# Mixing the blocks of one weight's Hadamard transform on GpSimd instead of TensorE, in a transformer layer's kernel

## The reference

```python
x = x + _layernorm(attn(_layernorm(x)))       # 16 heads of 32, rotary on all of q and k
x = x + _layernorm(ffn(_layernorm(x)))
# ffn, with n = 512, INTER = 2048:
x = fwht(x * SU_ug) / SCALE
x_up = x @ W_up.T * (Wscale_ug[:INTER] * SCALE)
x_gate = x @ W_gate.T * (Wscale_ug[INTER:] * SCALE)
x = jax.nn.silu(x_gate) * x_up
x = fwht(x * SU_dp) / SCALE
x = x @ W_down.T * (Wscale_dp * SCALE)
```

## Time and profile before

| what | us |
|---|---|
| median of 3 runs (1948.71 to 1949.36) | 1949.24 |
| time of the profiled execution | 1946.86 |
| its span | 1944.8 |
| PE busy | 1845.8 |
| DVE busy | 1263.3 |
| ACT busy | 1159.8 |
| POOL busy | 940.5 |

### The profile page before, as it was taken

One profiled execution on the slowest core, in us unless ns is written; L12 is line 12 of the kernel. 1 busy time (PEld: TensorE's weight loads), 2 busy tenths in 40 slices (PEclk: granted clock), 3 DMA queues, 4 the chain that ended last, 5 costly groups with the idle time before them and its releaser, 6 DMA issues.

```text
span 1944.8 us, 45513 instructions
## 1 busy us (share of the span) xinstructions
PE 1845.8 (95%) x18248; PEld 1282.4 (66%) x18248; DVE 1263.3 (65%) x2477; ACT 1159.8 (60%) x2003; POOL 940.5 (48%) x990
## 2 busy tenths in 40 slices
...
GB/s 245 248 99 132 157 55 61 99 142 93 72 88 145 91 98 126 98 126 99 89 114 142 87 73 93 135 100 99 118 106 126 99 88 107 112 76 77 119 84 71
DMA packets 353009, 213.23 MB, mean 110 GB/s; under 512 B 285216, under 2 KB 286496, under 8 KB 351776
## 3 DMA queue, kind: packets, MB, share of 16 engines
...
## 4 chain that ended last, share of the span: by engine, by line
PE 73%; DVE 8%; ACT 6%; POOL 4%; issue 4%; DMA 3%; SPq 1%; POOLq 0%; ACTq 0%; DVEq 0%
PE ps L900 29%; PE ps L925 15%; PE ps L846 5%; PE ps L836 5%; PE ps L857 5%; PE ps L873 4%; PE ps L892 2%; PE ps L747 2%; PE ps L878 2%; DVE mx L1385 2%; PE ps L805 2%; ACT pr L1076 1%; POOL rs L1470 1%; DMA qT<-tok 1%; POOL pr L1496 1%
## 5 line engine op out<-in xcount | busy, mean ns | idle before, releaser
L1076 ACT ACTIVATE pr<-ps,exp_scale 128x512 f16<-128x512 f32 x512 | 352.0, 688 | 262.1 <-PE ps L857 252.9
L1496 POOL TENSOR_TENSOR pr<-p,pr 128x512 f16<-128x512 f32 x256 | 296.4, 1158 | 326.5 <-ACT p L1082 326.4
L1385 DVE TENSOR_REDUCE mx<-ps 128x1 f32<-128x512 f32 x512 | 333.2, 683 | 97.7 <-PE ps L846 95.6
L900 PE MATMUL ps<-x2T,gate_w 128*128 128x256 f16 x3072 | 377.5, 273 | 0.0
L900 PE MATMUL ps<-x2T,up_w 128*128 128x256 f16 x3072 | 377.2, 273 | 0.0
L925 PE MATMUL ps<-room 128*128 128x512 f16 x1536 | 363.4, 379 | 0.2
L1399 DVE TENSOR_TENSOR pr<-ps,pr 128x512 f16<-128x512 f32 x256 | 176.1, 688 | 257.8 <-ACT ps L1087 257.5
L900 PEld LDWEIGHTS ps<-x2T,gate_w 128*128 128x128 f16 x3072 | 298.1, 98 | 56.7 <-issue 4.4
L900 PEld LDWEIGHTS ps<-x2T,up_w 128*128 128x128 f16 x3072 | 300.2, 98 | 43.2
L1524 POOL TENSOR_TENSOR room<-room 128x256 f16<-128x256 f32 x256 | 170.9, 676 | 273.2 <-ACT room L1112 272.9
L925 PEld LDWEIGHTS ps<-room 128*128 128x128 f16 x1536 | 148.4, 98 | 158.3 <-POOL room L1524 6.2
...
## 6 DMA issues: line engine op xcount, KB each, us to landing
room<-down_mid SPq DMA_DIRECT2D x256, 256.0 KB, 3.0
...
x2T<-in_W_gate SPq DMA_DIRECT2D x5, 1024.0 KB, 5.8
gate_w<-in_W_down SPq DMA_DIRECT2D x4, 1024.0 KB, 7.5
```

Source lines behind the costliest of these rows:

```text
L900: mm = nc.tensor.matmul(ffn_ps[i % 2][:, half * HALF:(half + 1) * HALF], weights[:, chunks[j // 4], kt, pw, j % 4 * P:(j % 4 + 1) * P], x2 ...
L1076: nc.scalar.activation(pr[:, p_buf(b, U), 0, 2 * j:2 * j + 2, :].rearrange("p h q -> p (h q)"), work[k], ACT.Exp, scale=exp_scale[:, 0:1]) ...
L1385: nc.vector.tensor_reduce(mx[:, t, h:h + 1], work[k], AX.X, ALU.max).then_inc(sm_freed.sem, 1)
L1496: nc.gpsimd.tensor_tensor(lo, p32[:], hi, ALU.subtract).then_inc(p_low.sem, 1)
```

## The change

After it, chunks 0 to 3 of W_down are loaded once, to the four parts of up_w. mx reads them there. A new POOL step bf does H(4) over m1 in fp32: for the widths 512 and 1024 it adds and subtracts halves, from `raw[k]` to `mid` and back, each time 1024 columns wide. cut then works on mixed numbers. dz has two matmuls. The halves from dyh and dyl go to a buffer of their own, `d_turned`, with two places. ldx.0 to 3 are gone; raw.0 to 3 wait for nothing. Chunks 4 and on use other buffers and waits, and all tables of order and of PSUM banks are new.

```diff
+MIX = (4 * P, 8 * P)
...
-        RAW_AT = [gate_part(2), gate_part(0), gate_part(1), gate_part(2), gate_part(0), gate_part(2), gate_part(0), gate_part(2),
-                  x2_16, gate_part(0), x2_16, x2_16]
-        CUT_AT = [up_part(c) for c in range(4)] + [gate_part(1), up_part(3), gate_part(1), up_part(3)] + [
+        RAW_AT = [up_part(c) for c in range(4)] + [gate_part(0), x2_16, gate_part(0), x2_16, gate_part(0), x2_16, x2_16, x2_16]
+        CUT_AT = [gate_part(2), up_part(0), up_part(1), up_part(2)] + [gate_part(1), up_part(3), gate_part(1), up_part(3)] + [
...
+        mid = gate_part(3).bitcast(F32)
...
+        d_turned = room[:, 3072:4096].bitcast(F16).rearrange("p (k i n) -> p k i n", k=2, i=2)
...
             def ldx(b, k):
-                if k >= 2:
+                if k >= 6:
                     sp.wait_ge(m_seen, k - 1)
...
             def raw_(b, k):
-                if k < 3:
-                    sp.wait_ge(a_lo, 4 * k + 4)
...
+                if k < 4:
+                    sp.dma_start(raw[k], chunk(k)).then_inc(d_in[k], 16)
...
             def dz(b, n):
-                pe.wait_ge(t_done, 4 * (n // 4) + 4)
-                mixed(n, n % 4)
+                pe.wait_ge(t_done, n + 1)
+                if n == 0:
+                    pe.wait_ge(bo_sum, 2)
+                if n >= 2:
+                    pe.wait_ge(q_done, n - 1)
+                for i in range(2):
+                    mm = nc.tensor.matmul(ps[:, 6 + n % 2, :], had[0], d_turned[:, n % 2, i, :], start=i == 0, stop=i == 1)
+                mm.then_inc(q_filled, 1)
...
             def cut_(b, k):
-                sc.wait_ge(r_loaded[k % 3], 16 * (k // 3 + 1))
-                sc.wait_ge(d_scaled if k < 4 else f_scaled, 1)
+                if k < 4:
+                    sc.wait_ge(d_mixed, k + 1)
+                    sc.wait_ge(d_scaled, 1)
+                    if k == 0:
+                        sc.wait_ge(a_lo, 4)
+                    if k:
+                        sc.wait_ge(d_lo, k)
...
             def mx_(b, k):
+                if k < 4:
+                    dve.wait_ge(d_in[k], 16)
...
+            def bf(b, k):
+
+                pool.wait_ge(d_in[k], 16)
+                for n, width in enumerate(MIX):
+                    src, dst = ((raw[k], mid), (mid, raw[k]))[n % 2]
+                    left, right = (src.rearrange("p (m i n) -> p m i n", i=2, n=width)[:, :, i, :] for i in range(2))
+                    both = dst.rearrange("p (m i n) -> p m i n", i=2, n=width)
+                    if n == 0 and k:
+                        pool.wait_ge(d_mixed, k)
+                    if n:
+                        pool.wait_ge(d_turn, (len(MIX) - 1) * k + n)
+                    if n == 1:
+                        pool.wait_ge(m_seen, k + 1)
+                    nc.gpsimd.tensor_tensor(both[:, :, 0, :], left, right, ALU.add)
+                    nc.gpsimd.tensor_tensor(both[:, :, 1, :], left, right, ALU.subtract).then_inc(
+                        d_mixed if n == len(MIX) - 1 else d_turn, 1)
```

The beginnings of the new FRONT of POOL, SP, ACT and PE (those of before in the first lines of each pair):

```diff
-        xs.0 xs.1 xs.2 xs.3 xn.0 xn.1 xn.2 xn.3 asl.0 asl.1 asl.2 asl.3 asl.4 xs.0@1 asl.5 asl.6 asl.7 asl.8
-        asl.9 asl.10 proj.0.0 ...
+        xs.0 xs.1 xs.2 xs.3 xn.0 xn.1 bf.0 xn.2 asl.0 asl.1 asl.2 asl.3 asl.4 asl.5 asl.6 xn.3 bf.1 asl.7 asl.8
+        asl.9 asl.10 asl.11 bf.2 proj.0.0 cut.0 tok.0.0 proj.0.1 cut.1 tok.0.1 bf.3 proj.1.0 cut.2 xs.0@1
+        tok.1.0 cut.3 proj.1.1 ...
...
-        xl.0 xl.1 lda.4 lda.2 ldv.2 xl.2 xl.3 lda.3 lda.1 lda.5 ldx.0 ldv.0 lda.0 ldx.1 ln1.0 xl.0@1 ln1.1 ldx.2
-        ln1.2 ln1.3 ldv.3 ldx.3 ...
+        lda.4 lda.2 xl.0 xl.1 xl.2 ldv.2 lda.3 lda.1 lda.5 xl.3 ldv.0 raw.0 lda.0 raw.1 ln1.0 raw.2 raw.3 ldv.3
+        ldv.4 ldx.4 xl.0@1 ln1.1 ln1.2 ldv.1 ldx.5 ln1.3 wput.0 ldx.6 xl.1@1 wget.0 ldx.7 ...
...
+        xn.0 xn.1 xn.2 ash.0 ash.1 ash.2 ash.3 ash.4 ash.5 ash.6 xn.3 arh ash.7 ash.8 ash.9 ash.10 brh ash.11
+        c.1 cut.0 tk.0.0 c.0 cut.1 tk.0.1 cut.2 v.0 v.1 tk.1.0 cut.3 ...
...
-        ... smax.0.15 warm.7 v.2 v.3 dy.0 warm.3 dy.1 st.0 st.1 dy.2 st.2 ...
+        ... smax.0.15 warm.4 proj.1.1 warm.10 v.2 v.3 st.0 st.1 dy.0 dy.1 dz.0 st.2 ...
```

More of the change, by code:

```diff
@@ L61 @@
     PE="""
[L62 to L85, removed]
+        smax.3.4 c.1@1 smax.3.5 av.18 av.19 smax.3.6 smax.3.7 c.0@1 smax.3.8 st.40 down.13@-1 down.14@-1 st.41
+        smax.3.9 down.15@-1 smax.3.10 smax.3.11 proj.0.0@1 st.42 gate.16@-1 st.43 up.16@-1 smax.3.12 smax.3.13
@@ L86 @@
+        st.37@1 up.14 av.16@1 av.17@1 st.38@1 st.39@1 gate.15 smax.3.1@1 down.12 smax.3.2@1 smax.3.3@1 up.15
     """,
     ACT="""
[L88 to L91, removed]
@@ L111 @@
[L111 to L115, removed]
@@ new lines @@
+        smax.0.6 smax.0.7 smax.0.8 smax.0.9 smax.0.10 smax.0.11 smax.0.12 smax.0.13 fmx smax.0.14 smax.0.15
+        mtok.0 xn.0@1 proj.1.1 v.2 v.3 dyl.0 low.0 dyl.1 low.1 dyl.2 dzl.0 dzl.1 smax.1.0 smax.1.1 dyl.3
+        smax.1.2 smax.1.3 smax.1.4 dzl.2 dyl.4 dzl.3 low.2 smax.1.5 smax.1.6 dyl.5 smax.1.7 fsc dyl.6 smax.1.8
+        dzl.4 dzl.5 low.3 dyl.7 proj.2.0 xs.2@1 dyl.8 dzl.6 dzl.7 low.4 smax.1.9 dyl.9 norm.0 smax.1.10
+        smax.1.11 smax.1.12 smax.1.13 smax.1.14 smax.1.15 dyl.10 proj.2.1 low.5 mtok.1 dzl.8 dyl.11 low.6 low.7
@@ L246 @@
+        norm.1@1 low.9@1 gelu.5 smax.2.0@1 low.10@1 smax.2.1@1 smax.2.2@1 smax.2.3@1 smax.2.4@1 gelu.6
+        smax.2.5@1 smax.2.6@1 smax.2.7@1 ys.3 smax.2.8@1 low.11@1 smax.2.9@1
     """,
     POOL="""
[L248 to L250 removed]
@@ L258 @@
+        proj.2.1@1 low.7@1 tok.2.1@1 hid.2 hid.3 norm.0@1 low.8@1 low.9@1 hid.4 hid.5 yn.2 ys.3 norm.1@1
     """,
     SP="""
-        xl.0 xl.1 lda.4 lda.2 ldv.2 xl.2 xl.3 lda.3 lda.1 lda.5 ldx.0 ldv.0 lda.0 ldx.1 ln1.0 xl.0@1 ln1.1 ldx.2
-        ln1.2 ln1.3 ldv.3 ldx.3 ldv.4 ldx.4 ldv.1 ldx.5 xl.1@1 raw.0 wput.0 ldx.6 wget.0 raw.1 ldx.7 stk.0.0
-        stk.0.1 raw.2 ldx.8 raw.3 ldx.9 ldx.10 ldx.11 stq.0 stk.1.0 stk.1.1 wput.1 wget.1 raw.4 dst.0 dst.1
-        dst.2 stq.1 rl.0 dst.3 dst.4 xl.2@1 raw.5 stk.2.0 stk.2.1 rl.1 dst.5 dst.6 ln1.0@1 ln1.1@1 xl.3@1 dst.7
```

376 lines of the change are left out of this document (206 added, 170 removed), and 13 rows, old and new, of tables (MIDDLE, UPPER).

## The result

The changed kernel takes 1953.32 us (median of 18 runs, 1952.67 to 1956.34), the kernel before 1949.45 beside it: ratio 1.0019, 95% interval 1.0013 to 1.0026. The forecast was 1939 us, a gain. The profiled execution took 1953.55, its span is 1951.7 (1944.8 before), 6.9 us longer. That is more than the 3.9 between the medians, because the profiled execution of the kernel before, 1946.86, was a quick one, 2.6 under its median.

What follows compares the result with a forecast made beforehand. PE was taken to bound the kernel, with ACT nearly full in the turning stage. Span 1944.8 - 17.1 (PE work) + 4.2 (start) + 3 (idle) + 0 (passes, tail) = 1934.9, about 10 us less: 1939 us, range 1926 to 1951.

Steps and rivals of the forecast that it cites:

- The start, step by step: Everything before the first attention scores (st): they come at 108.4 us against 104.2, 4.2 us later, range -2 to +12.
- (1): Start, loads of x: tile 3 queues behind three weights; xn.0 and xn.1 on POOL end near 22.8, not 21.3.
- (2): Start, first mixing on POOL: raw.0 lands about 24 us, bf.0 runs 24 to 33.5, xn.2 ends at 34.7 (30.25 before).
- (3): Start, SP's load order: ln1.1 lands about 43, xn.3 ends at 44.8, c.1 starts near 50 (39.93 before).
- (4): Start, POOL's further list: bf.1, bf.2 and cuts; W_down's scales ready near 65, tok.0.1 done at 84 (67.3 before).
- I take no such cost: bf's adds on POOL: no slowing while DVE reads; 18% on every add would make one bf 1.7 us longer.
- the turning stage: First scores to first gate product: PE work 210 us, ACT 204, 3 us more idle time, bounds -5 and +12.
- C: Turning stage: ACT holds its present length but for 6.5 us of work moved behind gate.0; 1948 us, chance 0.13.
- D: POOL's adds: 4.1 us each, one bf 16.4, first scores 21 us later than reckoned; 1960 us, chance 0.06.
- E: The six passes: their new order brings waits of a few us each; 3 us per pass gives 1957, chance 0.12.
- F: Start: DVE and POOL hinder each other, 18% per add, 5 us before the first smax; 1944 us, chance 0.06.
- B: Start and turning stage: full gain of 20.7 and up to 5 us more, start not later; 1927 us, chance 0.17.

Runs made afterwards that it cites:

- e5: Changed kernel with the load of x's tile 3 directly behind tile 2 in SP's queue: 1948.43 us, 0.9994 of the kernel before.
- e13: Changed kernel without bf's adds and subtracts and with x's tile 3 loaded directly behind tile 2: 1940.16 us, 0.9954 of the kernel before.
- e3: Changed kernel with eight matmuls in each dz again instead of two: 1965.70 us, 1.0086 of the kernel before.
- e11: Changed kernel without ACT's scaling of the rows of W_up and W_gate: 1952.49 us, 1.0013 of the kernel before.
- e12: Changed kernel without ACT's scaling of W_up and W_gate and with eight matmuls in each dz: 1963.27 us, 1.0069 of the kernel before.
- e4: Changed kernel without bf's adds and subtracts and with eight matmuls in each dz: 1957.31 us, 1.0042 of the kernel before.
- e1: Changed kernel without bf's sixteen adds and subtracts on POOL: 1944.28 us, 0.9974 of the kernel before.
- e9: Changed kernel with x's tile 3 loaded early, bf's adds in 256-column pieces and POOL's low halves in 512-column pieces: 1946.81 us, 0.9982 of the kernel before.
- e10: Changed kernel with x's tile 3 early, adds and low halves in pieces, and chunk 6 loaded ahead of the write of W_down's scales: 1945.44 us.
- e8: Kernel before the change with POOL's low half of each weight cut in four pieces of 512 columns: 1947.02 us, 0.9982 of the kernel before.

## Why the prediction was wrong

**What failed is "The start, step by step".** It gave 4.2 us, with -2 to +12 as bounds; 18.7 were measured. These 14.5 us are as much as the whole miss (1953.3 - 1939 = 14.3). In its order:

- (1) took the late x tile as 1.5 us on POOL's xn.1. POOL's xn.1 ended at 25.6, not 22.8, and the tile held DVE too, ahead of everything on its list: xs.3 began 3.9 us later than before. In the chain the tile is worth 4.1 to 4.9 us of the time (e5, e13).
- (2) let bf.0 run through. It stood 5.57 us for mx.0, a wait that the diff shows. xn.2 ended at 41.6, not 34.7; (3) put c.1 at 50, it came at 57.0. Half of the miss is there already.
- (4) had W_down's scales ready at 65 and tok.0.1 at 84; they came at 81 and 99.3. I followed POOL's list alone, and took DVE's, which went from 82.9 to 93.8 us of busy time, as given. "I take no such cost" is the term that was put at nothing: the spread of L1496 showed that POOL isn't lengthened, and said nothing of DVE, which is. (In the changed kernel POOL's instruction is the late one once, 2.673 us against 2.34, at 74.30.) A row of before had it: 4.016 us for 16 columns.
- From tok.0.1 to st (5) the forecast was 24.4 and the run 23.6; (6), dy not late, held.

**Right in its sum, wrong in its parts: the turning stage.** Forecast 241, measured 243.6. PE's idle time was forecast at 28.5 + 3 and stayed at 28.9, by two changes that nearly cancel and that the forecast hadn't worked out: the new lists saved 5.0 us of it (e3), and the missing dz matmuls opened 5.4 us of gaps. That is most of why these matmuls gave 10.8 to 13.0 us, not 20.7. That the sum came out is luck. PE's work came to 210.4 where the clock didn't fall (e11), against 210 forecast, and to 214.7 where it did.

**The rivals.** C (ACT sets the stage) is refuted by e11: 17 us less of ACT for 0.8 us. D is refuted by the adds' 2.35 us, E by the passes. F named the meeting of DVE and POOL, but priced it on POOL's side, at 5 us and with 0.06; it was on DVE's. B needed a start that isn't later. The passes, the tail and POOL's time (+40.5 us) went as forecast; PE's busy time fell by 12.8, not 20, in these two executions, whose granted clock was 0.990 and 0.986. Between e12 and e11, which differ in the 96 matmuls alone and have nearly the same granted clock (0.986 and 0.987), the difference is 20.4.

**The account.** 1949.5 + 4.5 (x tile) + 3.3 (other loads and lists) + 8.4 (adds) - 12.4 (dz) = 1953.3: e4 is 7.8 over before, of which the x tile is 4.1 (e1 - e13) to 4.9 (changed - e5); adds and dz are e3 - e4 and e3 - changed. The 3.3 are a remainder: a later start, less waiting in the turning stage, and the 2.7 us behind the first gate. How much of the adds' 8 to 9 us is DVE held and how much POOL's own time isn't settled: pieces of 256 columns give back 3.3 us of the start and 4.9 of DVE's 11.1 us.

**No version gains from the change for certain.** e9 and e10 beat both kernels (0.9982 and 0.9984), but e8, the old kernel with POOL's low halves in pieces, has 0.9982 as well.
